# Attention with a gated residual: the gate moved into the reciprocals, the sum to GpSimd, its statistics to the next step

## The chip, the cores and the metric

The kernel runs on one core of a Trainium2 chip. The metric is the time on the device in microseconds (us), the median of several executions. The core has five engines with queues of their own that go on side by side and meet at semaphores: PE (TensorE, matrix products), DVE (VectorE), ACT (ScalarE), POOL (GpSimd) and SP (SyncE, which here only issues DMAs). PEld is the loading of PE's weights.

## The reference

64 batches of 128 tokens with 256 values each pass through a gated cross attention and then through a mixture of experts:

```
x = x + tanh(g_xattn) * attention(layernorm(x), ctx, ctx, mask)      # 16 heads of 16 values
x = x + tanh(g_ffn) * ffn(layernorm(x))                              # 8 experts, each takes its best tokens
```

The attention is a softmax over 128 keys for each head and batch. The ffn chooses for each expert the 1024 tokens with the highest scores of all 8192, so nothing of it can start before the last batch has left the attention.

## The kernel before

The kernel has two blocks, `attention` and `choose_and_run`, each with a hand-written program for every engine. The order of the work on an engine is the order of the code. In `attention` four batches make a group; `steps` goes through all batches b in order (with 16 more steps at the end in which the pipeline runs empty), and `b.j` is the place of b in its group, 0 to 3. Each engine runs its own `step(b)`, and `b.back(n)` is the batch of n steps ago. A batch is in the pipeline for five steps:

- Step b: PE's `scores` makes the scores of batch b a first time (`a_ps`, two banks, in two halves per step), DVE's `maximum` takes the row maxima out of them (L665, four per step: two before and two after the other work of the step). PE's next half waits until DVE has emptied the banks.
- Step b+1: the maxima are transposed, ACT negates them (L534), and SP sends them by DMA into the stacked queries (`max_rows`, L340).
- Step b+2: PE makes the scores again, with the maxima in them (`b_ps`; it waits here for that DMA, `s_m`), and ACT takes the exponential (L527).
- Step b+3: PE's `values`, ACT's copy `o_t`, and PE's `out_back` (L970), which transposes the result into the single bank `o_ps`; column 16 of each head is the sum of the exponentials.
- Step b+4: DVE's `finish(b)`: the reciprocals of the sums (L739), the division into `o_n` (L742), gate times `o_n` plus residual rows into `x2` (L750), and the mean and variance of `x2` (L754, L757).

Beside this, PE's `front` makes queries, keys and values of the next group in eight parts. When a group's four rows of statistics are there, POOL's `ln2_scales` makes 16 small dependent operations of them (L416 to L428), ACT's `normalise2` (L547) uses these, and then come the router's products and the scores by which experts choose. `ln1` does the same for the input's normalisation.

SP's queue is in order too. This is its step, and two waits that matter for the change:

```python
if b.j == 0:
    residual(g)          # wait(sp, x2_done, g.times(4, -4)), then load x_res
    load_x(g.on(2)); load_c(g.on(2)); load_mask(g.on(2))
if b.j == 1:
    store_x2(g.on(-2))
if b.j == 3:
    store_rows(g.on(-3))
max_rows(b.back(1))
...
# PE, out_back(b), use = b.back(3): the bank o_ps must have been read
wait(pe, ot_out, use.times(1))
# PE, scores(b, x), at x == 0: the maxima must have landed in the queries
pe.wait_ge(s_m[back.s % 2], back.turn(2, 16, 16))
```

`x2_done` counts the batches whose `x2` is written, `ot_out` those whose `o_n` is written.

Of the kernel before, what the change touches and what calls it, by code (L numbers as in the profile page):

```python
# [30 lines left out]
ALU = mybir.AluOpType  # L31
# [3 lines left out]
P = 128  # L35
D = 256
HEADS = 16
DH = 16
# [3 lines left out]
VW = 32  # L42
# [108 lines left out]
def attention(nc, ctx, w, x, ctx_t, mask, g_x, wq, bq, wk, bk, wv, bv, wg_t, out, rows, scores_t,  # L151
# [42 lines left out]
    neg_m = [sb(f"neg_m{i}", [HEADS, P]) for i in range(2)]  # L194
    p_t = [sb(f"p_t{i}", [P, HEADS, P]) for i in range(2)]
    o_t = [sb(f"o_t{i}", [P, 4, P]) for i in range(2)]
    rden, o_n = sb("rden", [P, HEADS]), sb("o_n", [P, D])

    x_res = [sb(f"x_res{p}", [P, GB, D]) for p in range(2)]
    x2 = [sb(f"x2_{p}", [P, GB, D]) for p in range(2)]  # L200
# [47 lines left out]
    s_const, s_turn, s_same_ps, s_same = sem("s_const"), sem("s_turn"), sem("s_same_ps"), sem("s_same")  # L248
    s_fold, s_ends, s_bcast, s_bound, s_low = sem("s_fold"), w["s_ends"], sem("s_bcast"), sem("s_bound"), w["s_low"]
    s_cut, s_top = w["s_cut"], w["s_top"]  # L250
    s_again = sem("s_again")
    expert_of, row_of = sb("expert_of", [E, P]), sb("row_of", [VW, P])

    def steps(eng, step):
# [23 lines left out]
    with nc.Block() as block:  # L278
# [124 lines left out]
        @block.gpsimd  # L403
        def _(pool):
            for p in range(2):
                pool.memset(v_aug[p][:], 0.0).then_inc(s_zero, 1)
            for p in range(2):
                pool.memset(k_st[p][:], 0.0).then_inc(s_ones, 1)
            pool.memset(ident[:], 0.0).then_inc(w["s_id"], 1)
            pool.wait_ge(w["s_id"], 1)  # L410
            pool.affine_select(out=ident[:], in_=ident[:], compare_op=ALU.not_equal, fill=1.0, base=0,
                               pattern=[[-1, P]], channel_multiplier=1).then_inc(w["s_id"], 1)

            def rsqrt(c, var, v, y, t):

                c.link(pool.tensor_scalar(v[:], var, EPS, None, ALU.add))  # L416
                c.link(pool.tensor_scalar(y[:].bitcast(I32), v[:].bitcast(I32), -0.5, MAGIC, ALU.mult, ALU.add))
                for _ in range(3):
                    c.link(pool.tensor_tensor(t[:], y[:], y[:], ALU.mult))
                    c.link(pool.tensor_tensor(t[:], t[:], v[:], ALU.mult))  # L420
                    c.link(pool.tensor_scalar(t[:], t[:], -0.5, 1.5, ALU.mult, ALU.add))
                    c.link(pool.tensor_tensor(y[:], y[:], t[:], ALU.mult))

            def scales(c, mv, v, y, t, nm):

                rsqrt(c, mv[:, :, 1], v, y, t)
                c.link(pool.tensor_tensor(t[:], mv[:, :, 0], y[:], ALU.mult))
                c.link(pool.tensor_scalar(nm[:], t[:], -1.0, None, ALU.mult))  # L428
                assert c.n == LN_OPS

            def ln1(g):
                if g.ok:
                    pool.wait_ge(s_mv1, g.times(4, 4))
                    wait(pool, s_xn, g.times(4))
                    scales(Chain(pool, s_ln1, g.times(LN_OPS)), mv1, v1, y1, t1, nm1)

            def ln2_scales(g):
                if g.ok:
                    pool.wait_ge(mv2_done, g.times(4, 4))
                    wait(pool, xn2_done, g.times(4))  # L440
                    scales(Chain(pool, ln2, g.times(LN_OPS)), mv2[g.p], v2, y2, t2, nm2)

            def context_lo(g):
                if g.ok:
                    wait(pool, f_done, g.times(8, -8))
                    for k in range(KD):
                        pool.wait_ge(ch_done, g.times(KD, k + 1))
                        pool.tensor_tensor(c_lo[g.p][:, k, :], c_t[:, k, :], c_hi[g.p][:, k, :].bitcast(F32), ALU.subtract).then_inc(cl_done, 1)

            def search_consts():  # L450

                c = Chain(pool, s_turn)
                c.link(pool.memset(in_turn[:], 1.0))
                c.link(pool.affine_select(out=in_turn[:], in_=in_turn[:], compare_op=ALU.is_ge, fill=0.0, base=0,
                                          pattern=[[-E, GB]], channel_multiplier=1))
                c.link(pool.affine_select(out=in_turn[:], in_=in_turn[:], compare_op=ALU.is_ge, fill=0.0, base=E - 1,
                                          pattern=[[E, GB]], channel_multiplier=-1))
                for i in range(CUTS):
                    pool.memset(nth[:, i:i + 1], i + 1.0).then_inc(s_const, 1)
                for r in range(ROUNDS):  # L460
                    pool.memset(powers[:, r:r + 1], (1.0 + 2.0 ** -20) / float(CUTS + 1) ** (r + 1)).then_inc(s_const, 1)

            context_lo(Group(0, 0, NG))
            ln1(Group(0, 0, NG))
            ln1(Group(0, 1, NG))
            context_lo(Group(0, 1, NG))

            def step(pool, b):
                g = b.group
                if b.j == 1:  # L470
                    ln1(g.on(2))
                if b.j == 2:
                    context_lo(g.on(2))
                if b.j == 0:
                    ln2_scales(g.on(-2))
                if at_last(b, NG, 0):
                    search_consts()

            steps(pool, step)
# [133 lines left out]
        def _(dve):  # L613
# [115 lines left out]
                dve.tensor_scalar(cuts[:, 0:CUTS], nth[:], steps_[:, 0:1], low[0][:, 0:1], ALU.mult, ALU.add).then_inc(s_cut, 1)  # L729
                dve.tensor_copy(cuts[:, SLOTS - 1:SLOTS], low[0][:]).then_inc(s_top, 1)  # L730

            def finish(b):

                if not b.ok:
                    return
                dve.wait_ge(ot_done, b.times(1, 1))
                o = o_ps[:].rearrange("p (h v) -> p h v", v=VW)
                wait(dve, ot_out, b.times(1))
                dve.reciprocal(rden[:], o[:, :, DH]).then_inc(rd_done, 1)  # L739
                dve.wait_ge(rd_done, b.times(1, 1))  # L740
                wait(dve, x2_done, b.times(1))
                dve.tensor_tensor(o_n[:].rearrange("p (h d) -> p h d", d=DH), o[:, :, 0:DH],  # L742
                                  rden[:].unsqueeze(2).to_broadcast([P, HEADS, DH]), ALU.mult).then_inc(ot_out, 1)
                dve.wait_ge(ot_out, b.times(1, 1))
                g = b.group
                dve.wait_ge(s_res[g.p], g.turn(16, 16))
                if b.j == 0:
                    wait(dve, s_out[g.p], g.turn(16))
                    wait(dve, xn2_done, g.times(4, -4))
                dve.scalar_tensor_tensor(out=x2[g.p][:, b.j, :], in0=o_n[:], scalar=gx[:, 0:1], in1=x_res[g.p][:, b.j, :],  # L750
                                         op0=ALU.mult, op1=ALU.add).then_inc(x2_done, 1)
                dve.wait_ge(x2_done, b.times(1, 1))
                wait(dve, mv2_done, b.times(1))
                dve.bn_stats(stats2[:], x2[g.p][:, b.j, :]).then_inc(st2_done, 1)  # L754
                dve.wait_ge(st2_done, b.times(1, 1))
                wait(dve, ln2, g.times(LN_OPS, -LN_OPS))
                dve.bn_aggr(mv2[g.p][:, b.j, :], stats2[:]).then_inc(mv2_done, 1)  # L757
# [21 lines left out]
            def step(dve, b):  # L779
# [8 lines left out]
                    make_k(f, 1)  # L788
                if b.j == 3:
                    make_v(f, 1)  # L790
                finish(b.back(4))
                if at_last(b, NG, 0):
                    again()
                maximum(b, 2)
# [979 lines left out]
```

## Time and profile before

| | us |
|---|---|
| median of 3 executions | 870.19 (869.41 to 872.29) |
| the profiled execution | 869.9 |
| its span in the trace | 868.2 |

Busy over the whole span: PE 755.3 us (87%), PE's weight loads 632.3 (73%), DVE 584.7 (67%), ACT 511.9 (59%), POOL 329.7 (38%). The attention takes the first 500 us or so of the span; what follows it is the search for the experts' thresholds, and the experts. A share over the whole span mixes these stages, so the attention is read by itself, in windows and in the timeline. In a timeline a row gives the start, the length and the operation; "x2" means two of them in a row, and the square bracket says how long the engine had been idle before it and what it is taken to have waited for.

### The profile page before, as it was taken

The page shows a single profiled execution, that of the slowest core. Times are in us where ns is not written, and L with a number is a line of the kernel's source. Part 1 is how long each engine was busy: PE and PEld are TensorE (multiplying, and loading weights), DVE is VectorE, ACT ScalarE, POOL GpSimd, SP SyncE. Part 2 cuts the span into 40 slices and gives each one's busy share as a digit, 9 for nine tenths or more (in the row PEclk, how much of TensorE's full clock was granted, in tenths as well). Part 3 has the DMA queues.
Part 4 walks back from the last instruction along what each step waited for, and adds up shares of the span by engine and source line. Part 5 has one row for each costly group of instructions (what it writes and reads, how often), then busy time and mean ns, then how long its engine had stood idle before and what let it go on. Part 6 is the DMA issues. An engine that isn't in the chain of part 4 may idle for free. (4 is left out here: it accounts for less than half of the span.)

```text
span 868.2 us, 24784 instructions
## 1 busy us (share of the span) xinstructions
PE 755.3 (87%) x9570; PEld 632.3 (73%) x9570; DVE 584.7 (67%) x1421; ACT 511.9 (59%) x1004; POOL 329.7 (38%) x729
## 2 busy tenths in 40 slices
PE   1699999999999999999998731499999999999993
PEld 1477778878877788777886620279888888888983
DVE  3368888887888788888877649765747456474440
ACT  3246577766766676667756637265555655556641
POOL 6221243313422342324301231345384654747505
PEclk9889999999999999999999955599999999999997
DMA  4423343344434442445222233145364453625314
GB/s 133 136 89 129 129 156 109 133 163 162 141 125 139 161 170 96 158 150 179 96 85 78 85 114 122 39 135 116 83 121 117 81 110 68 136 45 86 38 13 49
DMA packets 76772, 97.06 MB, mean 112 GB/s; under 512 B 8264, under 2 KB 55880, under 8 KB 76616
## 3 DMA queue, kind: packets, MB, share of 16 engines
q1 hardware_dynamic: 64368, 78.44, 26.9%
q0 software_dynamic: 12288, 17.05, 12.3%
q8 instruction: 77, 1.26, 0.7%
q14 instruction: 39, 0.32, 0.1%
HBM read 52.37 MB, written 25.72 MB: 90 GB/s over the span
## 5 line engine op out<-in xcount | busy, mean ns | idle before, releaser
L665 DVE TENSOR_REDUCE m_sb<-a_ps 128x4 f32<-128x512 f32 x256 | 162.8, 678 | 51.6 <-PE a_ps L886 43.8
L527 ACT ACTIVATE p_t<-b_ps 128x512 f32<-128x512 f32 x256 | 143.5, 588 | 67.3 <-PE b_ps L894 67.2
L886 PE MATMUL a_ps<-k_st,q_st 31*128 31x128 f32 x2048 | 150.4, 285 | 28.5 <-ACT p_t L527 14.3
L886 PEld LDWEIGHTS a_ps<-k_st,q_st 31*128 31x128 f32 x2048 | 126.5, 188 | 54.9 <-issue 38.9
L894 PE MATMUL b_ps<-q_st,k_st 32*128 32x128 f32 x2048 | 148.5, 283 | 1.2 <-ACT p_t L527 1.0
L1204 POOL DMA_INDIRECT out<-y,idx_add x64 | 100.3, 1567 | 110.7 <-ACT y L1263 88.4
L894 PEld LDWEIGHTS b_ps<-q_st,k_st 32*128 32x128 f32 x2048 | 124.2, 186 | 2.1 <-issue 1.4
L416 POOL TENSOR_SCALAR v<-mv 128x4 f32<-128x4 f32 x32 | 7.2, 226 | 304.9 <-issue 147.1
L1573 PE MATMUL bank<-x_hi,w_hi 128*128 128x512 f32 x254 | 100.1, 394 | 0.0
L1441 DVE TENSOR_TENSOR act_h<-act_h,bank 128x512 f32<-128x512 f32 x64 | 44.0, 687 | 83.3 <-PE bank L1573 80.6
L1573 PE MATMUL bank<-x_lo,w_hi 128*128 128x512 f32 x254 | 99.0, 390 | 0.0
L1573 PE MATMUL bank<-x_hi,w_lo 128*128 128x512 f32 x254 | 98.9, 389 | 0.0
L1195 POOL DMA_INDIRECT xg<-rows_scratch,idx x64 | 68.2, 1066 | 56.2 <-DVE idx L1398 37.3
L1251 ACT ACTIVATE act_h<-bank 128x512 f32<-128x512 f32 x64 | 38.4, 599 | 72.7 <-PE bank L1573 72.1
L1614 PE MATMUL bank<-w_hi,hid_hi 128*128 128x256 f32 x256 | 74.8, 292 | 0.0
L1614 PE MATMUL bank<-w_hi,hid_lo 128*128 128x256 f32 x256 | 71.4, 279 | 0.0
L1614 PE MATMUL bank<-w_lo,hid_hi 128*128 128x256 f32 x256 | 71.3, 278 | 0.0
L911 PE MATMUL pv_ps<-p_t,v_aug 128*32 128x128 f32 x2048 | 69.2, 276 | 0.7 <-ACT xn_t L554 0.7
L540 ACT ACTIVATE o_t<-pv_ps 128x512 f32<-128x512 f32 x64 | 38.2, 597 | 45.3 <-PE pv_ps L911 45.2
L911 PEld LDWEIGHTS pv_ps<-p_t,v_aug 128*32 128x32 f32 x2048 | 52.0, 109 | 16.3 <-issue 12.6
L1263 ACT ACTIVATE y<-bank,weight 128x256 f32<-128x256 f32 x64 | 30.2, 472 | 46.8 <-PE bank L1614 46.5
L1573 PEld LDWEIGHTS bank<-x_hi,w_lo 128*128 128x128 f32 x254 | 47.7, 188 | 10.1
(237 smaller groups left out, 1726.7 us busy)
## 6 DMA issues: line engine op xcount, KB each, us to landing
w<-in_w_t SPq DMA_DIRECT2D x24, 512.0 KB, 4.8
rows_scratch<-xg SPq DMA_DIRECT2D x16, 528.0 KB, 3.0
x_in<-in_x SPq DMA_DIRECT2D x16, 512.0 KB, 5.0
c_t<-in_ctx_t SPq DMA_DIRECT2D x16, 512.0 KB, 5.8
k_st<-k_val SPq DMA_DIRECT2D x64, 128.0 KB
q_st<-q_val SPq DMA_DIRECT2D x64, 128.0 KB, 2.1
x_res<-in_x SPq DMA_DIRECT2D x16, 512.0 KB, 3.9
out<-x SPq DMA_DIRECT2D x16, 512.0 KB, 5.3
```

The lines of the kernel that those rows point to most:

```text
L527: act.activation(p_t[b.s % 2][:, 4 * r:4 * r + 4, :], b_ps[q % 2][:].rearrange("p (h s) -> p h s", s=P), ACT.Exp, scale=SCALE).then_inc(ex ...
L540: act.activation(o_t[b.s % 2][:], pv_ps[:].rearrange("p (a s) -> p a s", s=P), ACT.Copy).then_inc(pv_out, 1)
L665: dve.tensor_reduce(m_sb[b.s % 2][:, 4 * q:4 * q + 4], a_ps[q % 2][:].rearrange("p (h s) -> p h s", s=P), AX_X, ALU.max).then_inc(max_done, 1)
L886: mm = pe.matmul(a_ps[i][:, t * P:(t + 1) * P], q_st[p][r:r + A_K, t, tok], k_st[p][r:r + A_K, t, tok], start=True, stop=True)
L894: mm = pe.matmul(b_ps[i][:, t * P:(t + 1) * P], k_st[p][r:r + B_K, t, tok], q_st[p][r:r + B_K, t, tok], start=True, stop=True)
L911: mm = pe.matmul(pv_ps[VW * i:VW * (i + 1), q * P:(q + 1) * P], v_aug[b.group.p][:, b.j, h, :], p_t[b.s % 2][:, h, :], start=True, stop=True)
L1195: pool.indirect_dma_start(xg[e % 2][:, st, :], None, rows[:, :], bass.IndirectOffsetOnAxis(ap=idx[e % 2][:, st:st + 1], axis=0)).then_inc( ...
L1204: pool.indirect_dma_start(out[:, :], bass.IndirectOffsetOnAxis(ap=idx_add[e % 2][:, st:st + 1], axis=0), y[st][:], None, compute_op=ALU.ad ...
L1251: act.activation(act_h[n % 4][:], h1_ps[n % 2][:, 0:SPAN], ACT.Silu).then_inc(silu_done, 1)
L1441: dve.tensor_tensor(act_h[n % 4][:], act_h[n % 4][:], h3_ps[n % 2][:, 0:SPAN], ALU.mult).then_inc(gate_done, 1)
L1573: mm = pe.matmul(ps[:, 0:SPAN], w_[e % 2][i][:, k, f], x_[e % 2][:, k, h * SPAN:(h + 1) * SPAN], start=(n == 0), stop=(n == len(passes_) - 1))
L1614: mm = pe.matmul(y_ps[st % 2][:, 0:D], h_[h][:, f, t], w_[e % 2][2][:, f, :], start=(n == 0), stop=(n == len(passes_) - 1))
```

## The change

`finish(b)` is cut in three. `divide(b)` keeps the reciprocals. `scale_out(b)` multiplies the 16 reciprocals per row with the gate into a new tile `rden_g`, then makes `o_n` with these, so that `o_n` holds the gated result. The sum with the residual rows is now a plain addition in POOL's program (`add_rows`), first thing in its step. `row_stats` takes mean and variance one step later, as `row_stats(b.back(5))`, and stands between the other two in DVE's program.

```diff
+            def add_rows(b):
+                if b.ok:
+                    g = b.group
+                    pool.wait_ge(ot_out, b.times(1, 1))
+                    pool.wait_ge(s_res[g.p], g.turn(16, 16))
+                    if b.j == 0:
+                        wait(pool, s_out[g.p], g.turn(16))
+                        wait(pool, xn2_done, g.times(4, -4))
+                    pool.tensor_tensor(x2[g.p][:, b.j, :], o_n[:], x_res[g.p][:, b.j, :], ALU.add).then_inc(x2_done, 1)
...
             def step(pool, b):
                 g = b.group
+                add_rows(b.back(4))
                 if b.j == 1:
                     ln1(g.on(2))
...
-            def finish(b):
+            def divide(b):
...
                 dve.reciprocal(rden[:], o[:, :, DH]).then_inc(rd_done, 1)
+
+            def scale_out(b):
...
                 dve.wait_ge(rd_done, b.times(1, 1))
+                dve.tensor_scalar(rden_g[:], rden[:], gx[:, 0:1], None, ALU.mult).then_inc(rg_done, 1)
+                dve.wait_ge(rg_done, b.times(1, 1))
                 wait(dve, x2_done, b.times(1))
+                o = o_ps[:].rearrange("p (h v) -> p h v", v=VW)
                 dve.tensor_tensor(o_n[:].rearrange("p (h d) -> p h d", d=DH), o[:, :, 0:DH],
-                                  rden[:].unsqueeze(2).to_broadcast([P, HEADS, DH]), ALU.mult).then_inc(ot_out, 1)
-                dve.wait_ge(ot_out, b.times(1, 1))
+                                  rden_g[:].unsqueeze(2).to_broadcast([P, HEADS, DH]), ALU.mult).then_inc(ot_out, 1)
+
+            def row_stats(b):
...
-                dve.scalar_tensor_tensor(out=x2[g.p][:, b.j, :], in0=o_n[:], scalar=gx[:, 0:1], in1=x_res[g.p][:, b.j, :],
-                                         op0=ALU.mult, op1=ALU.add).then_inc(x2_done, 1)
                 dve.wait_ge(x2_done, b.times(1, 1))
                 wait(dve, mv2_done, b.times(1))
                 dve.bn_stats(stats2[:], x2[g.p][:, b.j, :]).then_inc(st2_done, 1)
...
-                finish(b.back(4))
+                divide(b.back(4))
+                row_stats(b.back(5))
+                scale_out(b.back(4))
```

DVE's program in a step with `b.j == 3`, from the reciprocals to the two maxima behind them, first of the kernel before:

```order
L739 RECIPROCAL rden<-o_ps 128x16 [waits ot_out,ot_done]
L742 TENSOR_TENSOR o_n<-o_ps,rden 128x256 [waits x2_done,rd_done]
L750 SCALAR_TENSOR_TENSOR x_0<-o_n,gx,x_res 128x256 [waits s_res0,ot_out]
L754 BN_STATS stats<-x_0 128x6 [waits mv2_done,x2_done]
L757 BN_AGGR mv_0<-stats 128x2 [waits ln2,st2_done]
L665 TENSOR_REDUCE m_sb<-a_ps 128x4 [waits a_done] x2
```

and of the changed one:

```order
L750 RECIPROCAL rden<-o_ps 128x16 [waits ot_out,ot_done]
L771 BN_STATS stats<-x_0 128x6 [waits mv2_done,x2_done]
L774 BN_AGGR mv_0<-stats 128x2 [waits ln2,st2_done]
L757 TENSOR_SCALAR rden_g<-rden,gx 128x16 [waits rd_done]
L761 TENSOR_TENSOR o_n<-o_ps,rden_g 128x256 [waits x2_done,rg_done]
L676 TENSOR_REDUCE m_sb<-a_ps 128x4 [waits a_done] x2
```

There are five operations between the maxima as before. The statistics (of the batch before) stand right behind the reciprocals, the sum is gone, and `o_n` comes last.

POOL's program from the context's rest (`c_lo`, at `b.j == 2`) to the start of `ln2_scales` (at `b.j == 0` of the next group), of the kernel before:

```order
L428 TENSOR_SCALAR nm<-t 128x4 [waits s_ln1]
L448 TENSOR_TENSOR c_lo<-c_t,c_hi 128x512 [waits ch_done,f_done,s_ln1]
L448 TENSOR_TENSOR c_lo<-c_t,c_hi 128x512 [waits ch_done]
L416 TENSOR_SCALAR v<-mv_1 128x4 [waits xn2_done,mv2_done]
L417 TENSOR_SCALAR y<-v 128x4 [waits ln2]
```

and of the changed one:

```order
L458 TENSOR_TENSOR x_0<-o_n,x_res 128x256 [waits s_res0,ot_out,s_ln1]
L448 TENSOR_TENSOR c_lo<-c_t,c_hi 128x512 [waits ch_done,f_done]
L448 TENSOR_TENSOR c_lo<-c_t,c_hi 128x512 [waits ch_done]
L458 TENSOR_TENSOR x_0<-o_n,x_res 128x256 [waits s_res0,ot_out]
L458 TENSOR_TENSOR x_1<-o_n,x_res 128x256 [waits s_out1,xn2_done,s_res1,ot_out]
L416 TENSOR_SCALAR v<-mv_0 128x4 [waits xn2_done,mv2_done]
```

An addition now stands ahead of each of POOL's pieces of work, one per step. PE's, ACT's and SP's programs are the same in both kernels.

## Rows read from the trace of the kernel before

**Rows 1.** Windows (start:end, us; busy us of each engine; granted clock): the attention's middle

```profile
240.00:300.00 60.00, 56.75 (x1013) 47.28 (x1012) 48.72 (x115) 40.52 (x84) 17.98 (x68) 1.00 0.42 146
```

**Rows 2.** Waits of PE from 60 to 480 us: total, times, longest

```profile
PE a_ps L886 <- ACT p_t L527: 13.5, 17, 1.3
PE a_ps L886 <- DVE m_sb L665: 8.3, 17, 0.9
```

**Rows 3.** PE's timeline (start, length, operation, idle before) at steps' starts

```profile
94.95 0.38 PE L886 MATMUL a_ps<-k_st,q_st 31*128 31x128 f32 x2 [0.86 <-ACT p_t L527]
101.67 0.38 PE L886 MATMUL a_ps<-k_st,q_st 31*128 31x128 f32 x2 [0.76 <-DVE m_sb L665]
...
213.64 0.38 PE L886 MATMUL a_ps<-k_st,q_st 31*128 31x128 f32 x2 [0.32 <-DVE m_sb L665]
...
242.43 0.38 PE L886 MATMUL a_ps<-k_st,q_st 31*128 31x128 f32 x2 [0.89 <-DVE m_sb L665]
...
262.48 0.60 PE L970 MATMUL o_ps<-ident,o_t 128*128 128x128 f32 x4
263.94 0.38 PE L886 MATMUL a_ps<-k_st,q_st 31*128 31x128 f32 x2 [0.86 <-ACT p_t L527]
...
467.12 0.38 PE L886 MATMUL a_ps<-k_st,q_st 31*128 31x128 f32 x2 [0.69 <-DVE m_sb L665]
```

**Rows 4.** DVE's timeline over `finish` and the maxima behind it

```profile
212.33 1.25 DVE L665 TENSOR_REDUCE m_sb<-a_ps 128x4 f32<-128x512 f32 x2
...
240.55 1.25 DVE L665 TENSOR_REDUCE m_sb<-a_ps 128x4 f32<-128x512 f32 x2
...
260.65 0.25 DVE L739 RECIPROCAL rden<-o_ps 128x16 f32<-128x16 f32 x1
260.93 0.42 DVE L742 TENSOR_TENSOR o_n<-o_ps,rden 128x256 f32<-128x256 f32 x1
261.39 0.48 DVE L750 SCALAR_TENSOR_TENSOR x<-o_n,gx,x_res 128x256 f32<-128x256 f32 x1
261.91 0.43 DVE L754 BATCH_NORM_STATS2 stats<-x 128x6 f32<-128x256 f32 x1
262.37 0.18 DVE L757 BATCH_NORM_AGGREGATE mv<-stats 128x2 f32<-128x6 f32 x1
262.47 1.25 DVE L665 TENSOR_REDUCE m_sb<-a_ps 128x4 f32<-128x512 f32 x2
```

**Rows 5.** ACT's timeline: the exponentials that PE's steps also wait for

```profile
262.49 1.06 ACT L527 ACTIVATE p_t<-b_ps 128x512 f32<-128x512 f32 x2
...
465.48 1.08 ACT L527 ACTIVATE p_t<-b_ps 128x512 f32<-128x512 f32 x2 [0.80 <-PE b_ps L894]
```

**Rows 6.** DVE's timeline: a short operation with a scalar per row

```profile
514.23 0.23 DVE L726 TENSOR_SCALAR steps<-powers,span_ 128x10 f32<-128x10 f32 x1
```

**Rows 7.** POOL's groups by form, 60 to 480 us: busy, mean ns | idle before

```profile
L448 POOL TENSOR_TENSOR c_lo<-c_t,c_hi 128x512 fp32r<-128x512 f32 x28 | 35.2, 1280 | 1.2
...
L419 POOL TENSOR_TENSOR t<-y 128x4 f32<-128x4 f32 x81 | 16.0, 198 | 6.5
```

**Rows 8.** SP's timeline: loads at a group's start, and the maxima

```profile
261.90 0.38 SPq L335 DMA_DIRECT2D x_res<-in_x  x1
...
265.95 0.59 SPq L340 DMA_DIRECT2D q_st<-neg_m  x1
```

**Rows 9.** DMA issues in 235.07:235.11, the mask's load: KB, us to landing

```profile
mask_b<-in_mask SPq DMA_DIRECT2D x1, 256.0 KB, 7.1
```

**Rows 10.** DMA issues in 206.5:206.55, the mask's load one group earlier

```profile
mask_b<-in_mask SPq DMA_DIRECT2D x1, 256.0 KB, 5.9
```

**Rows 11.** The attention's end: DVE's timeline

```profile
497.84 0.18 DVE L757 BATCH_NORM_AGGREGATE mv<-stats 128x2 f32<-128x6 f32 x1
```

**Rows 12.** The attention's end: POOL's timeline

```profile
498.12 0.23 POOL L416 TENSOR_SCALAR v<-mv 128x4 f32<-128x4 f32 x1 [9.67 <-DVE mv L757]
...
503.52 0.23 POOL L428 TENSOR_SCALAR nm<-t 128x4 f32<-128x4 f32 x1
```

More of the change, by code:

```diff
@@ L196, in attention @@
     o_t = [sb(f"o_t{i}", [P, 4, P]) for i in range(2)]
-    rden, o_n = sb("rden", [P, HEADS]), sb("o_n", [P, D])
+    rden, rden_g, o_n = sb("rden", [P, HEADS]), sb("rden_g", [P, HEADS]), sb("o_n", [P, D])
     x_res = [sb(f"x_res{p}", [P, GB, D]) for p in range(2)]
@@ L250, in attention @@
     s_cut, s_top = w["s_cut"], w["s_top"]
-    s_again = sem("s_again")
+    s_again, rg_done = sem("s_again"), sem("rg_done")
     expert_of, row_of = sb("expert_of", [E, P]), sb("row_of", [VW, P])
@@ L739, in finish @@
                 dve.reciprocal(rden[:], o[:, :, DH]).then_inc(rd_done, 1)
+            def scale_out(b):
+                if not b.ok:
+                    return
                 dve.wait_ge(rd_done, b.times(1, 1))
+                dve.tensor_scalar(rden_g[:], rden[:], gx[:, 0:1], None, ALU.mult).then_inc(rg_done, 1)
+                dve.wait_ge(rg_done, b.times(1, 1))
                 wait(dve, x2_done, b.times(1))
+                o = o_ps[:].rearrange("p (h v) -> p h v", v=VW)
                 dve.tensor_tensor(o_n[:].rearrange("p (h d) -> p h d", d=DH), o[:, :, 0:DH],
-                                  rden[:].unsqueeze(2).to_broadcast([P, HEADS, DH]), ALU.mult).then_inc(ot_out, 1)
-                dve.wait_ge(ot_out, b.times(1, 1))
+                                  rden_g[:].unsqueeze(2).to_broadcast([P, HEADS, DH]), ALU.mult).then_inc(ot_out, 1)
+            def row_stats(b):
+                if not b.ok:
+                    return
                 g = b.group
[L746 to L749, printed above, removed]
-                dve.scalar_tensor_tensor(out=x2[g.p][:, b.j, :], in0=o_n[:], scalar=gx[:, 0:1], in1=x_res[g.p][:, b.j, :],
-                                         op0=ALU.mult, op1=ALU.add).then_inc(x2_done, 1)
                 dve.wait_ge(x2_done, b.times(1, 1))
```

## The prediction

> **What bounds the kernel now.** I read the windows first, to see which engine fills the stage that the change touches. In the attention's middle PE is busy 56.75 of 60 us at the full granted clock, DVE 48.72, ACT 40.52 and POOL 17.98 [rows 1]. So the attention goes at PE's pace, and all that a faster DVE can give back is PE's idle time, some 22 us in all: the table of PE's waits has 13.5 us put down to ACT's exponentials and 8.3 us to DVE's maxima [rows 2]. Then PE's timeline, to see where these lie. They stand at the starts of steps alone, in a fixed pattern [rows 3]: at the start of `b.j == 0` PE is idle 0.86 us (263.94; 13 such rows from 94.95 on, and one of another length at either end), at that of `b.j == 1` 0.32 us (213.64; 11 such rows), but 0.76 in the first two groups (101.67) and 0.89 once (242.43).
>
> Who ends each of these waits is read by setting ends against starts. At `b.j == 1` the maxima end at 212.33 + 1.25 = 213.58 [rows 4] and PE starts at 213.64: DVE, 0.06 later. At `b.j == 0` the maxima end at 263.72 [rows 4], the exponentials at 263.55 [rows 5], PE starts at 263.94. The table names ACT, but DVE was later, and PE is 0.22 behind DVE in all fifteen. So DVE ends this wait too, with ACT close behind it. At 242.43 it was neither: the maxima had ended at 241.80 [rows 4]. PE's program there waits for one more thing, the DMA that puts the negated maxima into the queries. It is issued on SP behind the loads of `x_res`, `x_in`, `c_t` and the mask, and the mask, issued at 235.08, took 7.1 us [rows 9], so it landed at 242.18. One group earlier it took 5.9 [rows 10] and landed at 212.4, with 1.2 us to spare. That wait is what the change may bring back.
>
> **DVE's part.** From the reciprocals' start to the first maximum behind `finish` it is 260.65 to 262.47, 1.82 us [rows 4]. For the new order I take pitches from the same rows. Statistics that need nothing of the reciprocals start before these end: the maximum starts 0.08 before the aggregation's end (262.37 + 0.18 against 262.47), so 0.25 - 0.08 = 0.17. Statistics to aggregation 0.46, aggregation to the next 0.10. The multiplication of 128x16 isn't in the trace; the nearest is L726, 128x10 with a scalar per row, 0.23 [rows 6], and 0.04 until the next dependent start (260.93 less 260.65 + 0.25 shows 0.03): 0.27. Its bounds are 0.18 (the aggregation) and 0.48 (the sum that it replaces). Then `o_n`, 0.42 less 0.08. Sum 0.17 + 0.46 + 0.10 + 0.27 + 0.34 = 1.34, so DVE is 0.48 us shorter in each step (0.27 to 0.57).
>
> - At `b.j == 0` ACT takes over. Its exponentials end 0.17 before the maxima, so PE gains at least 0.09 and at most 0.25, by whether ACT's release has the short delay or the long one: 0.17 in 14 groups, 0.4 in the one at 94.95, together 2.8 us.
> - At `b.j == 1` the whole 0.33 could go, and 0.48 in the first two groups: 11 x 0.33 + 0.96 = 4.6 us, if the maxima's DMA allows it (below).
> - While the pipeline runs empty PE waits for DVE at 467.12 (0.69) and in two more steps [rows 3]. There ACT ends at 465.48 + 1.08 = 466.56 [rows 5], so 0.4 of each can go, less in the third: 1.0 us.
>
> **POOL's part.** An addition of 128x256 isn't there; that of 128x512 takes 1.28 us and that of 128x4 0.20 [rows 7], by a line between them 0.74 (bounds 0.64, half the larger, and 1.28). POOL has 42 of 60 us idle [rows 1], so this costs nothing by itself; what matters is who waits for `x2`. The next statistics come a step later, and even an addition held up behind `ln1`'s 16 operations is done before. `ln2_scales` starts a step later and still ends steps ahead of ACT's use, except at the end.
>
> **SP's part.** SP's `residual` waits for `x2` of the batch before. It went out at 261.90, right behind the sum's end at 261.87 [rows 4, 8]. Now `o_n` ends 1.42 after the reciprocals' start, at 262.07; 0.1 to POOL (498.02 to 498.12, [rows 11, 12]), 0.74 for the addition, 0.03 to SP: 262.94. The four loads, 1.8 MB, all go out 1.04 us later (0.8 to 1.6), and the maxima's DMA, issued at 265.95 as before [rows 8], lands behind them. At 242.43 PE started 0.25 after the mask had landed. With that distance the ordinary group has its maxima at 212.4 + 0.2 = 212.6; 1.04 later that is 213.7, where PE started at 213.64 and could now start at 213.3 - 0.17 = 213.15. So in the bad case the gap at `b.j == 1` isn't closed and swallows the gain at `b.j == 0` as well (and 0.1 more); in the good case it closes: the maxima are 8 KB in few pieces, and need not wait for the mask's last piece. I take half: 11 x 0.25 of the 11 x 0.50 that both gaps offer are lost, 2.7 us.
>
> **The end of the attention.** Nothing hides work here: the last batch's statistics, POOL's 16 operations, ACT, the router and the search stand in one chain. Before, the aggregation ends 1.90 us after the reciprocals' start (260.65 to 262.37 + 0.18 [rows 4]), here at 498.02 [rows 11]. Now `o_n` ends after 1.42, then 0.1 + 0.74 + 0.1 for POOL and back, 0.46 + 0.18 for the statistics: 3.0, so 1.1 us later (0.9 to 1.8).
>
> *A page that speaks against it.* POOL's row of 1.28 us for 512 columns [rows 7] is to be compared with DVE's 0.48 for the sum of 256 [rows 4]. The Trainium skill, GPSIMD Engine Reference, "Engine selection", says to keep two-input elementwise work on VectorE, since GpSimd is about twice as slow. By twice 0.48 the addition would take 0.96 and the end 0.2 us more than in my sum; the advice as such would speak against the move everywhere, while the rows say that POOL's time is on a path only at the end and through SP.
>
> **The sum.** 2.8 + 4.6 + 1.0 - 2.7 - 1.1 = 4.6 us less. The profiled execution took 869.9 for a span of 868.2; 869.9 - 4.6 = 865.3. The median of the runs shown is 0.3 above that execution: 865.6.
>
> **The rivals.**
> - *The loads swallow it* (no change). The maxima land behind the mask in every group, all of the gains at both starts in 11 groups are absorbed, and 0.1 lost in each: 2.8 + 4.6 - 11 x 0.6 + 1.0 - 1.1 = 0.7 less, 869.5. For it: 242.43. Against it: in one group of fourteen only.
> - *Each group becomes like 242.43* (slower). PE then starts 0.56 later at `b.j == 1` than before, 11 x 0.56 = 6.2, with 0.9 + 0.96 + 1.0 gained elsewhere and 1.1 lost: 3.4 to 4.5 us more, about 874. It takes loads 1.6 us later: an addition of 1.28 does it. It decides once the shift passes 1.1 us.
> - *All gaps close*: 2.8 + 4.6 + 1.0 - 1.1 = 7.3 less, 862.9. For it: POOL's addition may be shorter and the maxima's 8 KB may not wait for the mask.
> - *DVE isn't shorter* (no change or a little slower). DVE has five operations per step before and after. If the small multiplication and the waits around it cost the 0.75 us that would use up the gain (0.27 + 0.48), nothing is left but the later end: 1.1 more, 871.3. No row shows an operation that small above 0.3.
>  The Trainium skill, VectorE: DVE Perf Modes, "Rules for kernel authors", says to minimise the count of chained operations; the count stays the same here, so by that rule alone this is the outcome. The rows' overlap of 0.08 us between independent neighbours and the short 128x6 aggregation speak for a gain all the same.
> - *The bank `o_ps`*. `o_n` ends 0.7 us later in the step, and PE's L970 must find it read: at 262.48 [rows 3] against 262.07, 0.4 to spare. With a multiplication of 0.48 it is 0.2. I give this 4 in 100 and half a us per group: 868.
>
> **Chances.** What I forecast (part of the gaps closed) 0.42, all closed 0.18, swallowed 0.16, no shorter DVE 0.08, slower through the loads 0.12, the bank 0.04. A measurement of this kernel tells 0.3%, 2.6 us. Faster by more than that: 0.36 + 0.18 + 0.03 = 0.57; slower: 0.13; the same: 0.30. The range reaches from the closed gaps with the short bounds (862.0) to between the swallowed and the slower case (872.5).
>
> **What the next profile would show.** Right: reciprocals to maximum 1.3 to 1.4 us; POOL's addition 0.7 to 0.8; `x_res` issued some 1.0 us later in the step; PE idle 0.6 to 0.75 at `b.j == 0` and 0 to 0.6, uneven, at `b.j == 1`; POOL's last `ln2_scales` 1.1 us further behind the last reciprocals. Wrong: gaps of 0.8 and more at `b.j == 1` with the maxima long done, or an addition above 1.0 us.

## The result, and the profile after

| | before | changed |
|---|---|---|
| median of 7 executions each, us | 870.93 (869.41 to 872.29) | 866.22 (865.26 to 868.34) |
| the profiled execution's span, us | 868.2 | 865.1 |

The ratio is 0.9944 with an interval of 0.9929 to 0.9958: faster by 4.7 us, or 0.56%, and the whole interval lies below 1. 865.6 us was predicted.

First the page of the changed kernel, its busy times, then the windows of the same 60 us as [rows 1]:

```profile
PE 757.8 (88%) x9570; PEld 634.3 (73%) x9570; DVE 556.9 (64%) x1421; ACT 512.0 (59%) x1004; POOL 375.3 (43%) x793
```

```profile
240.00:300.00 60.00, 57.67 (x1040) 47.70 (x1033) 44.83 (x113) 40.99 (x86) 26.05 (x88) 1.00 0.41 139
```

DVE has given 3.9 us of 60 away and POOL has taken 8.1, and PE is busy 0.9 us more. PE still sets the pace. What it waits for, 60 to 480 us (total, times, longest), beside [rows 2]:

```profile
PE a_ps L905 <- ACT p_t L538: 10.8, 19, 1.0
PE a_ps L905 <- issue: 2.8, 9, 0.8
PE a_ps L905 <- DVE m_sb L676: 1.3, 3, 0.7
```

The names in this table are inferred by the profile, and ends set against starts correct one of them below. The waits put down to DVE fell from 8.3 to 1.3 us, those put down to ACT from 13.5 to 10.8, and 2.8 us are new, under "issue": the profile shows nothing that PE waits for there. DVE's timeline over the cut `finish` (start, length, operation), to be set against [rows 4]:

```profile
264.50 0.24 DVE L750 RECIPROCAL rden<-o_ps 128x16 f32<-128x16 f32 x1
264.66 0.37 DVE L771 BATCH_NORM_STATS2 stats<-x 128x6 f32<-128x256 f32 x1
265.06 0.18 DVE L774 BATCH_NORM_AGGREGATE mv<-stats 128x2 f32<-128x6 f32 x1
265.16 0.20 DVE L757 TENSOR_SCALAR rden_g<-rden,gx 128x16 f32<-128x16 f32 x1
265.40 0.42 DVE L761 TENSOR_TENSOR o_n<-o_ps,rden_g 128x256 f32<-128x256 f32 x1
265.74 1.28 DVE L676 TENSOR_REDUCE m_sb<-a_ps 128x4 f32<-128x512 f32 x2
```

From the reciprocals to the first maximum it is 1.24 us, 1.82 before. The count of operations is the same; what changed is who waits. Before, four of the five started behind the end of the one ahead, whose result they need. Now two do (the aggregation at 265.06 and `o_n` at 265.40); the statistics at 264.66 and `rden_g` at 265.16 start 0.08 before the operation ahead has ended. And `rden_g` takes 0.20 where the sum took 0.48. PE's timeline at starts of steps, five of `b.j == 0` (149.43, 260.91, 289.42, 429.71, 457.31) and four of `b.j == 1`, beside [rows 3]:

```profile
101.32 0.38 PE L905 MATMUL a_ps<-k_st,q_st 31*128 31x128 f32 x2 [0.74 <-DVE m_sb L676]
...
149.43 0.38 PE L905 MATMUL a_ps<-k_st,q_st 31*128 31x128 f32 x2 [0.63 <-ACT p_t L538]
...
156.12 0.38 PE L905 MATMUL a_ps<-k_st,q_st 31*128 31x128 f32 x2 [0.30 <-issue]
...
260.91 0.38 PE L905 MATMUL a_ps<-k_st,q_st 31*128 31x128 f32 x2 [0.63 <-ACT p_t L538]
...
268.15 0.38 PE L905 MATMUL a_ps<-k_st,q_st 31*128 31x128 f32 x2 [0.83 <-issue]
...
289.42 0.38 PE L905 MATMUL a_ps<-k_st,q_st 31*128 31x128 f32 x2 [0.63 <-ACT p_t L538]
...
408.42 0.38 PE L905 MATMUL a_ps<-k_st,q_st 31*128 31x128 f32 x2 [0.18 <-issue]
...
429.71 0.38 PE L905 MATMUL a_ps<-k_st,q_st 31*128 31x128 f32 x2 [0.63 <-ACT p_t L538]
...
457.31 0.38 PE L905 MATMUL a_ps<-k_st,q_st 31*128 31x128 f32 x2 [1.02 <-ACT p_t L538]
```

At `b.j == 0` the 0.86 became 0.63 in twelve groups, and PE (260.91) now starts 0.14 behind the exponentials and 0.34 behind the maxima:

```profile
259.28 1.29 DVE L676 TENSOR_REDUCE m_sb<-a_ps 128x4 f32<-128x512 f32 x2
...
259.70 1.07 ACT L538 ACTIVATE p_t<-b_ps 128x512 f32<-128x512 f32 x2
```

At `b.j == 1` the even 0.33 became uneven. From 120 us on three groups have no listed gap, eight have 0.16 to 0.37 and one has 0.83; of the two groups before them, which had 0.76 each, the first has none and the second 0.74. The maxima in front of the 0.83 end at 265.74 + 1.28 = 267.02, 1.13 before PE starts: it isn't DVE any more. Nor is it at 101.32, though the table names DVE: the maxima there ended at 100.73, 0.59 before. SP's timeline shows what moved (beside [rows 8]), and POOL's the addition it waits for:

```profile
260.02 0.38 SPq L335 DMA_DIRECT2D x_res<-in_x  x1
...
261.70 0.47 SPq L304 DMA_DIRECT2D mask_b<-in_mask  x1
262.93 0.59 SPq L340 DMA_DIRECT2D q_st<-neg_m  x1
```

```profile
259.26 0.73 POOL L458 TENSOR_TENSOR x<-o_n,x_res 128x256 f32<-128x256 f32 x1 [3.74 <-DVE o_n L761]
```

`x_res` goes out behind the addition's end at 259.99, 2.16 us after this step's reciprocals (257.86), where it was 1.25. So the four loads are 0.91 later in the step. The maxima's DMA goes out when ACT's negation is ready (262.90 here, 262.93 the DMA), so it follows the mask more closely: by 1.23 here and some 1.4 in most groups, where it was 1.77 (264.18 to 265.95) and 2.5 in most.

The end of the attention, on DVE and then on POOL, beside [rows 11, 12]:

```profile
491.26 0.25 DVE L750 RECIPROCAL rden<-o_ps 128x16 f32<-128x16 f32 x1
...
493.42 0.43 DVE L771 BATCH_NORM_STATS2 stats<-x 128x6 f32<-128x256 f32 x1 [0.84 <-POOL x L458]
493.88 0.18 DVE L774 BATCH_NORM_AGGREGATE mv<-stats 128x2 f32<-128x6 f32 x1
```

```profile
492.67 0.72 POOL L458 TENSOR_TENSOR x<-o_n,x_res 128x256 f32<-128x256 f32 x1 [3.12 <-DVE o_n L761]
494.15 0.23 POOL L416 TENSOR_SCALAR v<-mv 128x4 f32<-128x4 f32 x1 [0.77 <-DVE mv L774]
...
496.14 0.57 POOL L419 TENSOR_TENSOR t<-y 128x4 f32<-128x4 f32 x1
...
499.56 0.23 POOL L428 TENSOR_SCALAR nm<-t 128x4 f32<-128x4 f32 x1
```

Reciprocals to `ln2_scales` is 2.89 us, where it was 2.00: 0.89 is the price of the trip to POOL and back.

**Where the time went, stretch by stretch.** The starts of the same PE operations in both traces, and what the prediction had for the stretch:

| PE's stretch, us | before | changed | difference | predicted |
|---|---|---|---|---|
| up to a group's first scores (67.63, 68.26) | 67.63 | 68.26 | +0.63 | -0.17 |
| to 122.26, 121.62 | 54.63 | 53.36 | -1.27 | -1.5 |
| eleven groups, to 433.40, 429.71 | 311.14 | 308.09 | -3.05 | -2.75 |
| pipeline running empty, to 488.18, 483.32 | 54.78 | 53.61 | -1.17 | -1.17 |
| end, to the first `ends` product (511.80, 507.84) | 23.62 | 24.52 | +0.90 | +1.1 |
| search and experts, to the span's end | 356.40 | 357.26 | +0.86 | none |

The four rows between the first and the last come to -4.6, by chance the very sum of the prediction, in which single terms are off by more (below). The first row can't be told from scatter: in the other kernels' traces the same operation starts between 67.7 and 70.4. The prediction had a gain of 0.17 at its end (67.63), but the wait there is 0.49 us in both traces. The last row is not of the change's making either, as far as the programs tell. Each column is a single execution, and the medians moved by 4.7 where these spans moved by 3.1.

### The profile page after: what moved, and what is told of

Same layout as the page of the kernel before. It is cut to its first block and busy times, and to the rows that moved or that the text cites. A ratio compares the mean times of both kernels' runs of the same rounds, so it can differ in the third digit from the quotient of the medians.

```text
span 865.1 us, 24848 instructions
## 1 busy us (share of the span) xinstructions
PE 757.8 (88%) x9570; PEld 634.3 (73%) x9570; DVE 556.9 (64%) x1421; ACT 512.0 (59%) x1004; POOL 375.3 (43%) x793
## 5 line engine op out<-in xcount | busy, mean ns | idle before, releaser
L458 POOL TENSOR_TENSOR x<-o_n,x_res 128x256 f32<-128x256 f32 x64 | 47.0, 734 | 194.9 <-DVE o_n L761 171.6
```

Of the source, the lines that this page charges most:

```text
L458: pool.tensor_tensor(x2[g.p][:, b.j, :], o_n[:], x_res[g.p][:, b.j, :], ALU.add).then_inc(x2_done, 1)
```

## The experiments

Every kernel here computes the whole reference; two (runs 3 and 4) make an addition twice. Each is compared with the kernel before on its own chip (871.9 us for runs 1, 2, 3 and 5; 872.8 for 4, 6, 8 and 9; 871.5 for 7 and 10 to 12), so ratios are to be compared, not times.

**1. The loads ahead of `x_res`.** The theory says that late loads hold the maxima's DMA at `b.j == 1`. Let SP issue three of the loads without waiting for the sum, and `x_res` behind the maxima:

```diff
                 if b.j == 0:
-                    residual(g)
                     load_x(g.on(2))
...
                 max_rows(b.back(1))
+                if b.j == 0:
+                    residual(g)
```

> The changed kernel, but SP issues the loads of x_in, c_t and the mask ahead of the residual rows' load, which now comes behind the maxima's DMA and alone waits for x2. Theory (the loads, held up by the wait for POOL's sum, delay the maxima's DMA): PE's gaps at b.j == 1, together 3.6 us in the changed kernel, close in every group, and the median falls by 3 to 3.6 us to 862.6 to 863.2, 0.9905 of the kernel before. Rival (the gaps put down to issue are PE's own, or another wait's): they stay at 0.2 to 0.8 us and the time stays at 866.

Measured: 861.9 us, ratio 0.9885 (0.9867 to 0.9903). PE's timeline has a gap at each group's start and no other from 120 to 424 us:

```profile
230.92 0.38 PE L906 MATMUL a_ps<-k_st,q_st 31*128 31x128 f32 x2 [0.63 <-ACT p_t L539]
258.54 0.38 PE L906 MATMUL a_ps<-k_st,q_st 31*128 31x128 f32 x2 [0.63 <-ACT p_t L539]
```

The distance between these rows is the best measure in this case, since it has all of a group's waits in it, those too small to be listed as well. It is 27.60 to 27.62 in all eleven groups here. In the changed kernel it is 27.8 to 28.5 (149.43 less 121.62 is 27.81, with no gap listed at `b.j == 1`; 289.42 less 260.91 is 28.51), before it was 28.21 to 28.24 in nine of eleven. Over eleven groups the mean is 28.28 before, 28.01 in the changed kernel and 27.61 here: the change could give 0.67 us per group and gave 0.27, and the late loads cost 0.4 per group, 4.4 us over the eleven and 5.1 by the medians. That is more than the 3.6 that all listed gaps at `b.j == 1` come to. The changed kernel has its own control: its last full group (429.71 to 457.31) issues `x_res` but none of the other three loads, since no batches are left to load, and it takes 27.60, as every group does here.

**2. The same order of loads in the kernel before.** Is it the order alone that helps?

> The kernel before with the same new order of SP's loads. Theory: there only one group's maxima were late, so only the one gap of 0.89 us at b.j == 1 shrinks to 0.32, 0.6 us less in all: no change that can be measured, 870. Rival (the order of the loads is worth something by itself, apart from the change): 867 to 868, the same 3 us as on the changed kernel.

Measured: 872.88 us, 1.0001 (0.9985 to 1.0016). Gaps of 0.87 and 0.33 as before; only the single 0.89 is gone. The order is worth nothing while DVE ends the wait, and 5 us when it doesn't.

**3. The addition twice.** Its time, not its presence, should matter. POOL makes it first into a spare tile:

```diff
+                    wait(pool, s_spare, b.times(1))
+                    pool.tensor_tensor(spare[:], o_n[:], x_res[g.p][:, b.j, :], ALU.add).then_inc(s_spare, 1)
+                    pool.wait_ge(s_spare, b.times(1, 1))
                     pool.tensor_tensor(x2[g.p][:, b.j, :], o_n[:], x_res[g.p][:, b.j, :], ALU.add).then_inc(x2_done, 1)
```

> The changed kernel with POOL's addition made twice, first into a spare tile, so that x2 is ready 0.8 us later and nothing changes on DVE's, PE's and ACT's programs. Theory: all four loads go out 0.8 us later, the maxima land as much later, and each of the 11 groups' gaps at b.j == 1 grows by 0.8 from 0.3 on average to 1.0 to 1.1; with 0.8 us more at the attention's end 875 to 876. Rival (the gaps have another cause): only the 0.8 us at the end, 867.

Measured: 881.61 us, 1.0105 (1.0085 to 1.0124), slower than before by 9.7 us and over what was expected by 6. The timeline of one group, three engines in order of time:

```profile
267.85 0.38 PE L909 MATMUL a_ps<-k_st,q_st 31*128 31x128 f32 x2 [0.63 <-ACT p_t L542]
...
269.28 0.47 SPq L305 DMA_DIRECT2D mask_b<-in_mask  x1
...
269.86 0.59 SPq L341 DMA_DIRECT2D q_st<-neg_m  x1
...
272.68 1.28 DVE L680 TENSOR_REDUCE m_sb<-a_ps 128x4 f32<-128x512 f32 x2
...
275.31 0.38 PE L909 MATMUL a_ps<-k_st,q_st 31*128 31x128 f32 x2 [1.07 <-issue]
```

`b.j == 0` is unchanged at 0.63. At `b.j == 1` PE is idle 0.94 to 1.83 in all twelve groups, 1.35 after the maxima's end here, and the maxima's DMA is issued straight behind the mask. This is the slower rival of the prediction, brought about by a longer addition. In the last full group, where no loads stand, the distance is 27.61 here too.

**4. The addition twice, with the loads first.** It parts the two readings of run 3: POOL's own time, or the loads behind it.

> The doubled addition on POOL together with the loads ahead of the wait for x2. Theory (POOL's time costs through SP's queue and at the end alone): as the run with the loads first, and 0.8 us more at the end, 862.7. Rival (the late x2 or POOL's own time also costs in another way, with 9 us of the doubled addition's 15 only partly the loads): 866 and more.

Measured: 863.58 us, 0.9901 (0.9882 to 0.992), with 27.58 to 27.62 per group as in run 1. The second addition costs 0.0161 of the time with the loads behind it (run 3 less the changed kernel, 14 us), and 0.0016 with the loads ahead (run 4 less run 1, 1.4 us, which is within the scatter; one more addition at the end is 0.7 of it). So nearly all of it comes through SP's queue, and POOL's own time costs nothing in the steady groups.

**5. The sum back on DVE**, as a plain addition behind `o_n`, the statistics still a step later:

```diff
-                add_rows(b.back(4))
...
+                dve.wait_ge(ot_out, b.times(1, 1))
+                dve.tensor_tensor(x2[g.p][:, b.j, :], o_n[:], x_res[g.p][:, b.j, :], ALU.add).then_inc(x2_done, 1)
```

> The changed kernel with the sum as a plain addition on DVE, directly behind o_n; gate in the reciprocals and statistics one step later are kept. Theory (the gain is DVE's length between the maxima, most of it from the sum's leaving DVE): reciprocals to next maximum 1.24 + 0.46 = 1.7 us against 1.82 before, gaps of 0.75 at b.j == 0 and 0.2 at b.j == 1, 2 us gained and 0.6 lost at the end: 868.5 to 869.5. Rival (it was the later statistics that freed DVE): 1.3 to 1.4 us, and 865 to 866.

Measured: 870.19 us, 0.9979 (0.9968 to 0.999). DVE's rows:

```profile
260.47 0.42 DVE L760 TENSOR_TENSOR o_n<-o_ps,rden_g 128x256 f32<-128x256 f32 x1
260.93 0.43 DVE L768 TENSOR_TENSOR x<-o_n,x_res 128x256 f32<-128x256 f32 x1
261.27 1.28 DVE L675 TENSOR_REDUCE m_sb<-a_ps 128x4 f32<-128x512 f32 x2
```

1.70 us from the reciprocals (259.57) to the maximum. Split from the gate, the sum is one operation more; without POOL that eats most of what the later statistics give.

**6. The statistics a step later, and nothing else**, from the kernel before: gate, sum and residual rows stay fused on DVE.

```diff
+                divide(b.back(4))
+                row_stats(b.back(5))
                 finish(b.back(4))
```

> The kernel before with only one part of the change: the statistics one step later, between the reciprocals and o_n; the gate and the sum stay in DVE's one operation, nothing goes to POOL. Theory (statistics fill the time in which o_n waits for the reciprocals, and x2 comes only 0.4 us later): reciprocals to next maximum 1.53 us, gaps of 0.63 and 0.05, loads 0.4 us later, 0.6 us lost at the end: 865.5 to 866.5 on this chip, where the kernel before takes 871.9, so as much as the whole change gave or more. Rival (the sum's move to POOL is what gives the gain, as the run with the sum on DVE seems to say): 870.

Measured: 866.86 us, 0.9934 (0.9919 to 0.9949), with 1.52 us from reciprocals (257.66) to maximum (259.18) and this in PE's timeline:

```profile
260.72 0.38 PE L900 MATMUL a_ps<-k_st,q_st 31*128 31x128 f32 x2 [0.63 <-ACT p_t L527]
...
267.38 0.38 PE L900 MATMUL a_ps<-k_st,q_st 31*128 31x128 f32 x2 [0.26 <-DVE m_sb L665]
```

One part of the change alone gives as much as the whole: the intervals overlap, and over eleven groups the mean is 27.90 us here and 28.01 in the changed kernel. ACT ends the wait at `b.j == 0` once DVE is 0.3 shorter, and the further 0.28 that the rest of the change buys has nothing to close there. The sum is later here too (`x_res` goes out 1.63 behind the reciprocals, 1.25 before), and from 120 us on four groups have a listed gap at `b.j == 1`, with PE 0.27 to 0.67 behind the maxima, though the profile names DVE.

**7. That, with the loads first.**

> The kernel before with two edits, nothing on POOL: the statistics one step later and the loads ahead of the wait for x2. Theory (with the loads out of the way DVE's shorter stretch is all that counts, and 0.3 us of it are enough, since ACT ends PE's wait at b.j == 0 and only 0.33 us stand at b.j == 1): the same as the changed kernel with the loads first, 0.9885 of the kernel before, or up to 1 us above it, 0.989 to 0.990. Rival (the sum on POOL is worth something by itself): 2 us and more above it, 0.992.

Measured: 864.9 us, 0.9911 (0.9895 to 0.9927). A group takes 27.72 to 27.76 (one 27.84) against 27.61 in run 1, and in run 11, which ran on this chip: the rest of the change, the gate's multiplication and the sum on POOL, is worth 0.13 us per group when the loads are out of its way, 1.6 us over twelve groups. The ratio lies between theory and rival, 0.0026 above run 1, but the intervals overlap, so the worth rests on the traces.

**8. The statistics in the same step**, behind `scale_out`, so that DVE waits for POOL's sum:

```diff
                 divide(b.back(4))
-                row_stats(b.back(5))
                 scale_out(b.back(4))
+                row_stats(b.back(4))
```

> The changed kernel with the statistics taken in the same step again, directly behind o_n, so that DVE waits in place for POOL's sum. Theory (the later step is what keeps that wait off DVE): reciprocals to next maximum 2.35 us (1.82 before) where POOL is free, and some 2 us more at b.j == 2, where POOL's 16 operations of ln1 stand ahead of the sum; 14 us from the first and up to 20 from the second: 885 to 905, slower than before. Rival (DVE has enough slack, the step of the statistics doesn't matter): 866 to 868.

Measured: 916.69 us, 1.0515 (1.0485 to 1.0545), slower than I gave it. The timeline, DVE at `b.j == 2`, PE at the start of the next step, and DVE in that step:

```profile
247.59 0.43 DVE L771 BATCH_NORM_STATS2 stats<-x 128x6 f32<-128x256 f32 x1 [3.34 <-POOL x L458]
...
249.46 0.38 PE L905 MATMUL a_ps<-k_st,q_st 31*128 31x128 f32 x2 [1.45 <-DVE m_sb L676]
...
254.84 0.43 DVE L771 BATCH_NORM_STATS2 stats<-x 128x6 f32<-128x256 f32 x1 [0.84 <-POOL x L458]
...
255.40 1.25 DVE L676 TENSOR_REDUCE m_sb<-a_ps 128x4 f32<-128x512 f32 x2
```

DVE stands 0.84 to 0.91 us at the sum in three steps of a group and 3.3 at `b.j == 2`, where `ln1`'s 16 operations stand ahead of the sum on POOL, with the maxima queued behind it. Both are waits that the theory had; a group takes 31.17 us, 2.9 more than before. Moving the sum off without moving its reader costs 5%.

**9. ACT's exponentials ahead of `normalise2`.** With the loads first, ACT ends what is left at `b.j == 0`. ACT's program at `b.j == 3`:

```diff
-                if b.j == 3:
-                    normalise2(g.on(-2), (2, 3))
                 exp(b.back(2), 2)
                 exp(b.back(2), 3)
+                if b.j == 3:
+                    normalise2(g.on(-2), (2, 3))
```

> The loads first, and on ACT at b.j == 3 the last two exponentials ahead of the two rows of normalise2 instead of behind them. Theory (at b.j == 0 it is now ACT's exponentials that end PE's wait, DVE's maxima being done 0.3 us earlier): the gap there falls from 0.63 to 0.3 to 0.4 us in 14 groups, 3.5 to 4 us, 858. Rival (what is put down to ACT there is the group's other work): 0.63 stays, 862.

Measured: 869.22 us, 0.9966 (0.9954 to 0.9979): a miss by 11 us. The gap did shrink, but by 0.14 alone, since DVE is next; and another opened:

```profile
261.58 0.38 PE L906 MATMUL a_ps<-k_st,q_st 31*128 31x128 f32 x2 [0.49 <-ACT p_t L539]
...
263.49 0.66 PE L864 MATMUL f_ps<-ident,xn 128*128 128x128 f32 x4 [0.53 <-DVE xn_lo L647]
```

`normalise2` had filled ACT's wait for the scores. Now ACT waits there, and `normalise2` stands between the exponentials and `xn_hi`; that makes DVE's `xn_lo` late, for which PE's bank `f_ps` waits. A group takes 28.20 us, against 27.61 in run 1.

**10. `normalise2` behind ACT's copies for `front` too** (the same edit as in run 9, but behind `xn_t_out`).

> The loads first, and on ACT at b.j == 3 the two rows of normalise2 behind both the exponentials and the copy xn_hi. In the run with the exponentials first PE's gap at b.j == 0 fell by 0.14 us, to where DVE ends it, but xn_hi came 0.6 us later and PE waited 0.53 us for DVE's rest of it. Theory: now only the gain stays, 0.14 us in 14 groups, 2 us less than with the loads first alone: 0.9865. Rival (the rows of normalise2 are late next, for the router's transposes at b.j == 0): 0.9885 or more.

Measured: 861.47 us, 0.9879 (0.9863 to 0.9896), 27.45 to 27.49 per group against 27.61. From a group's first scores to the `ends` product the trace is 2.1 us shorter than in run 1, but the medians agree within their scatter.

**11. Only the last batch's sum on DVE.** This takes back the price at the end (run 1, and there `add_rows` leaves the last batch to DVE, with its statistics in the same step, and those of the batch before it are taken a step earlier).

> The changed kernel with the loads first, and at the attention's end the last batch's sum on DVE and the statistics of the batch before it taken in the idle time of the step before. Theory (0.9 us of the chain at the end are POOL's sum and these statistics): last reciprocals to the start of POOL's last 16 operations 2.0 us instead of 2.9, and 0.9 us less than with the loads first alone, 0.9875. Rival (something else is late next at the end): no change.

Measured: 861.61 us, 0.988 (0.9863 to 0.9896). Reciprocals to `ln2_scales` is 2.20 us (487.51 to 489.71) instead of 2.89, and the attention is 0.9 shorter in the trace; the medians of runs 1, 10 and 11 can't be told apart.

**12. Runs 1, 10 and 11 together, and the folds held back.** POOL's operations of 0.2 us took 0.57 in the middle of the last `ln2_scales` while DVE was folding the scores, work that isn't urgent there. DVE waits with it until `ln2_scales` is done:

```diff
                     dve.wait_ge(r_out, NG - 2)
+                    dve.wait_ge(ln2, LN_OPS * NG)
```

> All together: loads first, ACT's rows last, the last sum on DVE, and DVE's folds of the scores held back until POOL's last 16 operations are done. In the profiles four of these operations take 0.31 to 0.58 us instead of 0.2 while DVE's fold with two operands in SBUF runs. Theory: the 16 operations end 1.1 us sooner, and with 2.0 and 0.9 us from the other two edits the time is 4 us below the loads first alone: 0.984. Rival (the folds are then late for the search, or the slow operations have another cause): 0.985 to 0.986.

Measured: 858.22 us, 0.9844 (0.9827 to 0.9862), the best of this study: 0.010 below the changed kernel's ratio, 8.7 us. POOL's timeline, the first, the last and one that had taken 0.57:

```profile
487.25 0.23 POOL L417 TENSOR_SCALAR v<-mv 128x4 f32<-128x4 f32 x1 [3.90 <-DVE mv L779]
...
488.96 0.20 POOL L420 TENSOR_TENSOR t<-y 128x4 f32<-128x4 f32 x1
...
491.49 0.23 POOL L429 TENSOR_SCALAR nm<-t 128x4 f32<-128x4 f32 x1
```

4.47 us for the sixteen, 5.64 in the changed kernel (494.15 to 499.79), and none above 0.23.

## Why the prediction was right, by its own steps

- **PE bounds, and only its idle time can be won.** The stretches say so: DVE gave 0.58 us in each of four steps per group, and the group became 0.27 shorter. Over the eleven groups PE's listed gaps fell from 13.6 to 9.7 us and the time by 3.05; the other 0.8 went into waits too short to be listed, as in the group from 121.62, which has no gap listed at `b.j == 1` and yet takes 27.81 where run 1 has 27.61. Run 4 says it of POOL.
- **DVE's step, 1.34 predicted, 1.24 measured.** The multiplication came to 0.24 with the wait behind it (265.16 to 265.40; 0.27 taken), and the statistics to 0.40 (0.46 taken): issued without a wait they last 0.37 us, where [rows 4] has 0.43. The rival in which DVE isn't shorter, because it has five operations as before, is dead.
- **`b.j == 0`, 0.17 predicted, 0.23 measured.** PE is 0.14 behind ACT now, so the wait fell nearly by the upper bound of 0.25. (For the lower bound, 0.09, no row was given.) That ACT is what ends it is borne out by run 9, where earlier exponentials brought 0.49.
- **`b.j == 1`: half of the gain lost to late loads.** The mechanism is shown by runs 1 to 4. The net of the eleven groups was near (3.05 us gained, 2.75 predicted), but by luck in part, as the next point shows. I took the loss as a coin's two sides, a group in which the gap closes or one that swallows all, and the trace shows neither but a spread. That the maxima wait for the mask's landing plus 0.25, which priced the bad case, is wrong: in all eleven groups from 122 us on PE starts before the mask has landed, by 0.02 to 1.5 us. At 402.49 the changed kernel issues a mask that takes 7.1 us (the second row below, from the DMA issues in 402.45:402.53) and so lands at 409.59, and PE's step starts at 408.42:

```profile
402.49 0.47 SPq L304 DMA_DIRECT2D mask_b<-in_mask  x1
```

```profile
mask_b<-in_mask SPq DMA_DIRECT2D x1, 256.0 KB, 7.1
```

 The 8 KB don't wait for the mask's last piece, as the prediction allowed, but they do wait for something in the loads' stream: run 3 held them up in all groups. The Trainium skill, DMA: Bandwidth & Descriptors, "Queues, rings and completion order", says that a copy is split over up to sixteen rings, each taken in order, and that completion isn't first in, first out. The trace agrees in that the later, smaller transfer, for which PE's step waits, is done at least 1.2 us before the earlier one. Which piece of which load holds it isn't to be seen in any row here, and stays open.
- **The size of that loss was too small, and luck covered it.** 2.7 us were taken; run 1 gave 5.1 (0.0059 of 871 us), of which 4.4 lie in the eleven groups. A part lies in waits too short to be rows, 0.2 us in a group such as 121.62 to 149.43. What could be gained was too small as well: 0.67 us per group (run 1) where 0.50 was taken, 1.9 us over the eleven. Of these 1.9 us, 0.7 come from the extra 0.06 at each `b.j == 0`, and 0.6 from the single gap of 0.89 at 242.43, of which only 0.33 was counted; the rest is in no row of its own. The two errors leave 0.3 us. The pipeline running empty is luck in the same way: -1.17 was the forecast and the result, but 0.62 of it is the last full group, with no loads in its way, and 0.55 the emptying, for which 1.0 was taken.
- **SP's shift, 1.04 predicted, 0.91 measured**, since `o_n` came 0.1 earlier. It stayed under the 1.1 from which I had every group slower; doubling the addition took the shift to 1.71 (2.96 behind the reciprocals), and the kernel was slower. So the point lies between 0.91 and 1.71; that it is 1.1 no run shows.
- **POOL's addition, 0.74 predicted by a line between two rows, 734 ns measured** (the group of 61 between 60 and 480 us):

```profile
L458 POOL TENSOR_TENSOR x<-o_n,x_res 128x256 f32<-128x256 f32 x61 | 44.8, 734 | 190.0 <-DVE o_n L761 166.7 <-issue 22.1
```

 DVE makes the same addition in 0.43 (run 5), so POOL takes 1.7 times as long. The Trainium skill, GPSIMD Engine Reference, "Engine selection", has about twice. The direction agrees, and so does the advice to keep such work on VectorE, up to a point: run 7 beside run 1 has the move, with the gate's multiplication that goes with it, worth 0.13 us per group, and only with the loads first.
- **The end, +1.1 predicted, +0.90 measured.** Right in kind; DVE's step was 0.10 shorter, and the way back from POOL 0.03 (493.39 to 493.42) where 0.1 was taken. Run 11 takes 0.7 of it back.
- **The bank `o_ps`** never showed: in the changed kernel L989 has no listed idle time before it up to the last batch, where it waits for ACT.

What the prediction did not see is whose gain it was. It costed the change as a whole; run 6 has the later statistics alone at 0.9934 and the whole change at 0.9944. Beyond that step, the gate's multiplication, the split sum and POOL bring a shorter DVE that is worth 0.13 us per group at best, and loads that go out later.

Still open: why PE starts 0.21 to 0.22 behind DVE at `b.j == 0` where DVE ends the wait, and 0.06 behind it at `b.j == 1`; what in the loads' stream holds the maxima; and whether runs 10 and 11 are worth their 1 to 2 us each by themselves, which only their sum in run 12 makes measurable.

## What to carry to other kernels

Before an operation goes to an idle engine, follow who waits for its result in every in-order queue: here the cost was neither on the engine that took it nor on the one that gave it, but on SP, where loads stood behind the wait for it and an 8 KB transfer behind the loads. Ask what each piece of a bundle does alone, since moving the reader one step on gave all of this one's gain. And measure a periodic kernel by the distance between the same instruction of one group and the next: it showed 0.13 us per group where the medians' intervals overlapped.

## What the runs showed of the hardware

- **POOL's small operations stretch while DVE runs one with two inputs in SBUF.** The 128x4 operations take 0.20 us, but 0.57 at 496.14 in the changed kernel and 0.58 behind it. DVE's row beside them, with the one ahead of it, and the same row in run 12, where POOL is done before it starts:

```profile
494.74 0.61 DVE L716 TENSOR_SCALAR sc<-xg,turn 128x384 f32<-128x384 f32 x1
495.39 1.93 DVE L718 SCALAR_TENSOR_TENSOR sc<-xg,turn,sc 128x384 f32<-128x384 f32 x3
```

```profile
492.50 1.93 DVE L718 SCALAR_TENSOR_TENSOR sc<-xg,turn,sc 128x384 f32<-128x384 f32 x3
```

 DVE's three take 1.93 us either way; POOL alone pays. Beside DVE's operation just before, with one such input (L716, 494.74 to 495.35), POOL's stay at 0.20. The Trainium skill, GPSIMD Engine Reference, "Key points", says that GpSimd shares its SBUF interfaces with VectorE, with contention when VectorE has two SBUF inputs, and the trace agrees.
- **A DVE operation is recorded as shorter when it needn't wait for the one ahead.** The statistics of 128x256 last 0.37 us issued behind the independent reciprocals (264.66; all 63 such in the changed kernel) and 0.43 behind a wait (493.42, and all 64 in the kernel before), and the multiplication of 128x16 0.20 against 0.23 in the same way in run 12. Why isn't shown.
